# Routing stage written out batch by batch: layer norm three batches ahead over three buffers, squares and lengths earlier

## What is computed

```python
xn = _layernorm(x, ln_gamma, ln_beta)
x_unit = _l2norm(xn, axis=-1)
mu_unit = _l2norm(mu, axis=0)
logits = jnp.einsum('bnd,des->bnes', x_unit * scale, mu_unit)
dispatch = jax.nn.softmax(logits, axis=1)
combine = jax.nn.softmax(logits.reshape(B, N, E * S), axis=-1).reshape(B, N, E, S)
slot_in = jnp.einsum('bnd,bnes->besd', xn, dispatch)
```

## Time and profile before

| what | us |
|---|---|
| three runs: median (lowest, highest) | 1210.41 (1207.87, 1211.22) |
| the profiled execution | 1208.01 |
| its span, first to last instruction | 1206.2 |
| of the span, the routing stage | about 963 to 1110 |

### The profile page before, as it was taken

How to read it: one execution, slowest core, us unless ns; L and a number is a source line. 1 busy time by engine, 2 the same in 40 slices (tenths; PEclk the granted TensorE clock), 3 DMA queues, 4 the chain that set the end, 5 groups by cost and what they waited for, 6 DMA issues and landing times. The chain is left out here.

```text
span 1206.2 us, 28505 instructions
## 1 busy us (share of the span) xinstructions
PE 1040.5 (86%) x8053; PEld 988.6 (82%) x8053; DVE 874.2 (72%) x2292; ACT 748.9 (62%) x2513; POOL 437.8 (36%) x753
## 2 busy tenths in 40 slices
PE   6779999999999998799999926888888747777998
PEld 6679999999999998799999925877787647666877
DVE  4567767777776766677777756999999677776656
ACT  3466666666666665433333307999999547777754
POOL 0132322222332221121121125766777466663015
PEclk9889999999999999899999966999999869999559
DMA  7678960000000000100000035555556010000113
GB/s 230 139 134 226 135 116 0 0 0 0 0 0 0 0 0 1 32 1 0 0 0 0 0 91 139 166 167 151 169 152 174 4 19 1 0 0 4 41 35 122
DMA packets 71575, 73.90 MB, mean 61 GB/s; under 512 B 23025, under 2 KB 63829, under 8 KB 71381
## 3 DMA queue, kind: packets, MB, share of 16 engines
q1 hardware_dynamic: 70692, 72.47, 24.0%
q10 hardware_dynamic: 816, 0.66, 0.2%
HBM read 41.52 MB, written 31.54 MB: 61 GB/s over the span
## 5 line engine op out<-in xcount | busy, mean ns | idle before, releaser
L776 POOL TENSOR_TENSOR att_prob<-att_ex,att_rinv 128x308 f32<-128x308 f32 x128 | 89.9, 702 | 216.1 <-DVE att_rinv L679 202.8
L1056 ACT ACTIVATE att_ex<-att_s_bank,att_mx 128x77 f32<-128x77 f32 x512 | 143.3, 339 | 13.7 <-DVE att_mx L1122 12.1
L1338 ACT ACTIVATE ffn_hid<-ffn_h_bank,ffn_b 128x256 f32<-128x256 f32 x128 | 60.8, 476 | 125.5 <-DVE ffn_hT_lo L1369 65.7
L638 ACT ACTIVATE att_ex<-att_s_bank,att_mx 128x77 f32<-128x77 f32 x512 | 125.0, 333 | 11.5 <-DVE att_mx L669 11.4
L646 ACT ACTIVATE att_qT<-att_q_bank 128x256 f32<-128x256 f32 x128 | 49.2, 385 | 101.0 <-PE att_q_bank L496 99.9
L702 DVE TENSOR_TENSOR att_pT_lo<-att_t_bank,att_pT_hi 128x512 fp32r<-128x512 f32 x128 | 88.3, 691 | 32.1 <-ACT att_pT_hi L616 31.7
L1196 POOL TENSOR_TENSOR att_prob<-att_ex,att_rinv 128x256 f32<-128x256 f32 x128 | 79.8, 623 | 73.1 <-DVE att_rinv L1137 73.1
L516 PE MATMUL att_s_bank<-att_keys,att_qT 128*128 128x154 f32 x512 | 95.0, 309 | 0.0
L616 ACT CAST att_pT_hi<-att_t_bank 128x512 fp32r<-128x512 f32 x128 | 75.0, 587 | 24.2 <-PE att_t_bank L526 19.3
L540 PE MATMUL att_o_bank<-att_pT_hi,att_vals_hi 128*128 128x256 f32 x256 | 82.9, 324 | 3.0 <-DVE att_oT_lo L683 2.0
L1309 PE MATMUL ffn_o_bank<-ffn_w_hi,ffn_hT_hi 128*128 128x256 f32 x256 | 74.5, 291 | 8.0 <-DVE ffn_hT_lo L1369 8.0
(11 more groups left out here) (275 smaller groups left out, 4126.1 us busy)
## 6 DMA issues: line engine op xcount, KB each, us to landing
att_qs<-q_dram SPq DMA_DIRECT2D x96, 128.0 KB, 2.8
ks_dram<-att_zeros SPq DMA_DIRECT2D x16, 462.0 KB, 5.9
att_ks<-ks_dram SPq DMA_DIRECT2D x16, 462.0 KB, 5.2
all_x<-in_x SPq DMA_DIRECT2D x4, 1024.0 KB, 7.7
att_vd<-vd_dram SPq DMA_DIRECT2D x16, 256.0 KB
q_dram<-att_qT_hi SPq DMA_DIRECT2D x16, 256.0 KB, 2.1
q_dram<-att_qT_lo SPq DMA_DIRECT2D x16, 256.0 KB, 2.1
out<-comb_y SPq DMA_DIRECT2D x16, 256.0 KB, 2.1
```

Of the source, the lines that this page charges most:

```text
L638: last = nc.scalar.activation(ex[t % RING][:, r, :], s_bank[t % 2][:, r * SK:(r + 1) * SK], ACT.Exp, bias=mx[t % 2][:, r:r + 1])
L776: nc.gpsimd.tensor_tensor(out, e, w, ALU.mult).then_inc(p_ready, 1)
L1056: last = nc.scalar.activation(ex[t % RING][:, r, :], s_bank[t % 2][:, r * SK:(r + 1) * SK], ACT.Exp, bias=mx[t % 2][:, r:r + 1], **total)
```

## The change

The arithmetic is the same; order, buffers and waits differ.

- No loop: `every_batch` calls a body `batch(f)` for f = 0 to 16 with plain numbers, so each wait is for a constant.
- xa has three buffers (`XR`). In body f, `normalise` and `affine` work on batch f+3 (before: f+2), `statistics` and `inverse_deviation` on f+4 (before: f+3). The stage's head has one more of each, and the inverse of the second length.
- ACT: `square` stands behind the first exponentials instead of the second ones, the copy to moe_comb behind `transposed_x`, `round_x` ahead of the copy to moe_slots.
- DVE: `normalise` stands behind disp_lo instead of ahead of the first maxima; `transposed_x` and the first `weigh` ahead of the second maxima; `statistics` and `invert_length` (of f+2) behind these.
- POOL: `lengths` ahead of `inverse_deviation`. PE: the transposes of x ahead of the second logits.

```diff
-        xa = [m.sb(f"xa{i}", [P, NC, D]) for i in range(2)]
+        XR = 3
+        xa = [m.sb(f"xa{i}", [P, NC, D]) for i in range(XR)]
...
+        def every_batch(eng, body):
+            for f in range(B + 1):
+                body(f)
...
-                if front:
-                    logits(f, i, 1)
-                if following:
+                if f + 1 < B:
                     transpose_x(f + 1)
-                if back:
-                    slot_inputs(f - 1, 1 - i)
+                if f < B:
+                    logits(f, f % 2, 1)
+                if f > 0:
+                    slot_inputs(f - 1, (f - 1) % 2)
...
+            ln.normalise(dve, 2, xg_ready, 1)
+            ln.statistics(dve, 3)
+            invert_length(1)
+            every_batch(dve, batch)
...
-                wait_apart(poolt, xu_ready, NC * (f - 1))
-                wait_apart(poolt, xas_ready, f - 1)
-                nc.gpsimd.tensor_tensor(xa[i][:, :, :], xg[:, :, :], beta[:, :].unsqueeze(1).to_broadcast([P, NC, D]),
+                wait_apart(poolt, xu_ready, NC * (f - 2))
+                wait_apart(poolt, xas_ready, f - 2)
+                nc.gpsimd.tensor_tensor(xa[f % XR][:, :, :], xg[:, :, :], beta[:, :].unsqueeze(1).to_broadcast([P, NC, D]),
                                         ALU.add).then_inc(xa_ready, 1)
...
+            def batch(f):
+                if f < B:
+                    split_x(f, f % 2)
+                if f + 3 < B:
+                    affine(f + 3, 0)
+                if f + 2 < B:
                     lengths(f + 2)
+                if f + 4 < B:
+                    ln.inverse_deviation(pool, f + 4)
...
+            affine(2, 0)
+            ln.inverse_deviation(pool, 3)
+            every_batch(pool, batch)
```

More of the change, by code:

```diff
@@ L1607, in round_x, with batch @@
                 act.wait_ge(xa_ready, f + 1)
-                nc.scalar.copy(xaS[i][0][:, :, :], xa[i][:, :, :]).then_inc(xas_hi, 1)
-            def batch(f, i, front, back, following, later, latest):
+                nc.scalar.copy(xaS[i][0][:, :, :], xa[f % XR][:, :, :]).then_inc(xas_hi, 1)
+            def batch(f):
                 g = f - 1
-                if following:
-                    unit(f + 1, 1 - i)
-                if back:
+                if f + 1 < B:
+                    unit(f + 1, 0)
+                if f > 0:
                     act.wait_ge(t_psum, 2 * g + 1)
@@ L1617, in batch @@
                     nc.scalar.copy(disp[0][:, :, :], t_bank[0][:, :].rearrange("p (q n) -> p q n", q=NC)).then_inc(disp_hi, 1)
-                if front:
+                if f < B:
                     exponentials(f, 0)
-                if back:
-                    act.wait_ge(t_psum, 2 * g + 2)
[L1622 to L1626, removed]
+                if f + 2 < B:
+                    square(f + 2, 0)
+                if f + 1 < B:
+                    transposed_x(f + 1, (f + 1) % 2)
+                if f > 0:
+                    act.wait_ge(t_psum, 2 * g + 2)
+                    nc.scalar.copy(st.comb[:, :, g, :], t_bank[1][:, :].rearrange("p (j n) -> p j n", j=EC)).then_inc(comb_stored, 1)
+                if f < B:
                     exponentials(f, 1)
-                if later:
-                    square(f + 2, i)
-                if back:
+                if f + 1 < B:
+                    round_x(f + 1, (f + 1) % 2)
+                if f > 0:
                     act.wait_ge(i_psum, g + 1)
[L1632 to L1635, removed]
+                    nc.scalar.copy(st.slots[:, :, g, :], i_bank[:, :].rearrange("p (c n) -> p c n", c=DC)).then_inc(slots_stored, 1)
             square(0, 0)
@@ L1752, in split_x, with batch @@
                 wait_apart(poolt, xas_hi, f + 1)
-                nc.gpsimd.tensor_tensor(xaS[i][1][:, :, :], xa[i][:, :, :], fp32_of(xaS[i][0][:, :, :]),
+                nc.gpsimd.tensor_tensor(xaS[i][1][:, :, :], xa[f % XR][:, :, :], fp32_of(xaS[i][0][:, :, :]),
                                         ALU.subtract).then_inc(xas_ready, 1)
[L1756 to L1763, removed]
+            def batch(f):
+                if f < B:
+                    split_x(f, f % 2)
+                if f + 3 < B:
+                    affine(f + 3, 0)
+                if f + 2 < B:
                     lengths(f + 2)
+                if f + 4 < B:
+                    ln.inverse_deviation(pool, f + 4)
             pool.memset(ones[:, :], 1.0).then_inc(const_ready, 1)
```

35 lines of the change are left out of this document (16 added, 19 removed).

## The result

| | before | changed |
|---|---|---|
| median (lowest to highest), us | 1210.41 (1207.87 to 1212.93), 5 runs | 1216.91 (1214.33 to 1222.69), 5 runs |
| ratio to before, 95% interval | | 1.0055, 1.003 to 1.008 |
| the profiled execution; its span | 1208.01; 1206.2 | 1216.08; 1214.3 |

The changed kernel is slower by 0.55%, by more than the 0.3% that a measurement of this kernel can tell from no change. The forecast was 1217, the range 1209 to 1223.

What follows compares the result with a forecast made beforehand. No engine is full; a chain of waits through several engines paces the routing batches. Prologue +3.8, loop and new order +2.6, tail +1.0 sum to +7.4, giving 1217.8 by the median; 1217 us was said, range 1209 to 1223.

Steps and rivals of the forecast that it cites:

- prologue, to unit 2: Head of the routing stage, up to batch 2's scaling of x on ACT: third layer norm delays batch 0, +3.8 us.
- loop written out: Routing stage: twelve batches at the peeled 7.51 us instead of 98.33 in all, order unchanged: -8.2 us.
- new order, twelve batches: Middle of the routing stage: batches take 8.41 us each because the first weighting is held, +10.8 us against written-out batches.
- tail: Last batches of the routing stage, 13 to 15, with allowance for held second weightings: +1.0 us.
- Weighting 0 is held: First weighting of a batch on DVE waits until 0.15 us behind POOL's shift: batch 8.41 us, unheld 7.36.
- a second weighting held by the split: Batches 12 to 14: POOL's split may delay DVE's second weighting, 0 to 0.5 us each, 0.3 taken in all.
- The terms at nothing: Routing parts costed at zero: early squares, third buffer, PE's transposes ahead of second logits, reciprocal deviation last on POOL.
- squares early: ACT's squares behind the first exponentials: removes the 0.80 us wait for the inverse length, costed at nothing.
- its cover of 1.1: Slack between the inverse length being done near 7.3 us and wanted at 8.41; without it the wait returns one for one.
- Not held: Rival: first weighting on DVE runs freely beside POOL's shift, batches 7.36 us, total 1204 us; chance 0.15.
- Weighting 1 held too: Rival: POOL's split also holds the second weighting in every batch, twelve at 8.86 us, total 1223 us; chance 0.07.
- Shorter hand-overs: Rival: first weighting held, but third layer norm gets in first and hand-overs are 0.25 us shorter a batch: 1213; chance 0.12.

Runs made afterwards that it cites:

- the maxima first: Changed kernel with the second maxima put back ahead of the low parts of x and the first weighting on DVE: 1196.52 us, ratio 0.9906; again 1199.14 us.
- the kernel with both edits: Changed kernel with the first softmax's exponentials in PSUM and the second maxima moved ahead of the first weighting on DVE: 1197.04 us, ratio 0.9914 to before.
- the kernel with the squares late: Changed kernel with second maxima ahead of the first weighting, and squares put back behind the second exponentials on ACT: 1209.01 us, ratio 0.9984 to before.

## Why the prediction was right, by its steps

| term, us | forecast | measured | from |
|---|---|---|---|
| prologue, to unit 2 | +3.8 | +3.6 | (993.77 - 970.9) - (991.21 - 971.93) |
| loop written out | -8.2 | -7.8 | 90.50 - 98.33 |
| new order, twelve batches | +10.8 | +10.8 | 101.32 - 90.50 |
| tail | +1.0 | +1.0 | 0.0 + 0.4 + 0.6, below |
| sum | +7.4 | +7.6 | the whole stage on PE, as above: +7.5 |

**Weighting 0 is held.** This was the choice that made the sign, and the nearest row was the right one: the form with one scalar is held like that with two. (The 890 of that row is a mean of two kinds: in the single records a first instruction that meets POOL's addition takes 1.37 to 1.38 and ends 0.15 behind it, the second of its pair takes 0.40.) The written-down layout against the batch from 1019.09:

| since the unit's start | forecast | measured |
|---|---|---|
| layer norm, free | 2.01 to 2.75 | 2.03 to 2.76 |
| POOL scale; shift | 2.82; 4.16 | 2.84; 4.21 |
| weighting starts; ends | 4.2; 5.86 | 4.22; 5.91 |
| second maxima end | 6.46 | 6.51 |
| second exponentials | 6.50 | 6.55 |
| next unit | 8.41 | 8.45 |

The 0.04 that is left comes in between POOL's scale and its shift (1.37 apart instead of 1.34), and everything behind the shift carries it: the end of POOL's instruction is where the batch is tied. The Trainium skill ("GPSIMD Engine Reference", 8. Key points) says that GpSimd contends with DVE instructions in a two-port mode. The trace agrees; how long DVE waits, to 0.15 behind POOL's end, is read off the rows.

**The loop** gave 7.8 of the 8.2 in the experiment: a written-out batch takes 7.54 rather than the 7.51 of the earlier trace rows.

**The prologue.** The third layer norm did wait for the deviation and did meet POOL's split; the weighting of batch 0 then met scale and shift. DVE and POOL there:

```profile
987.17 1.69 DVE L351 TENSOR_SCALAR route_xn<-all_x,route_mean_var,route_rstd 128x256 f32<-128x256 f32 x2 [2.05 <-POOL route_rstd L343]
...
989.50 2.21 DVE L1673 TENSOR_SCALAR route_weight<-route_ex,route_rinv 128x256 f32<-128x256 f32 x2
991.63 0.68 DVE L1662 TENSOR_REDUCE route_top<-route_l_bank 128x2 f32<-128x512 f32 x1
```

```profile
987.10 1.28 POOL L1757 TENSOR_TENSOR route_xaS_lo<-route_xa,route_xaS_hi 128x512 fp32r<-128x512 f32 x1
988.94 1.27 POOL L1738 TENSOR_TENSOR route_xg<-route_xn,route_gamma 128x512 f32<-128x512 f32 x1 [0.55 <-DVE route_xn L351]
990.28 1.28 POOL L1744 TENSOR_TENSOR route_xa<-route_xg,route_beta 128x512 f32<-128x512 f32 x1
```

Normalise 3 (987.17, 1.69) stands in front of batch 0 and is held by the split, which starts 0.07 before it. The pair of the weighting (989.50, 2.21) is held twice, by the scale and by the shift, and ends 0.15 behind the latter.

**The tail** has the right sum from parts of which two were off. Batch 13 takes 7.36 as forecast (1102.45 - 1095.09), batch 14 6.43 to the copy at 1108.88 (forecast 6.40): 0.0 and +0.4. Batch 15 takes 4.50 to the copy at 1113.38, against 3.92 before (1102.95 to 1106.87): +0.6, forecast +0.4. The 0.3 set aside for a second weighting held by the split did not come: those pairs take 0.61 to 0.62. There it is POOL that pays (last section).

**The terms at nothing.** The unit's wait for the inverse is gone, as said. But "squares early" is worth nothing only under a cover, by the forecast that of the held weighting: with it gone (the maxima first) it is worth 0.39 a batch, and there it is still the inverse that the unit waits for. The changed kernel itself with the squares late was not run. The clause that the wait for the inverse would come back if its cover of 1.1 were gone was right in kind; that it comes back one for one was not measured.

**The rivals.** *Not held* (1204): refuted by the 1.69 of the pair, and by the kernel with the exponentials in PSUM, which shows what that case looks like: 7.61 a batch, of which 0.25 is the slower pair itself (0.86 less 0.61), and the rest, 7.36, is what this rival was laid out at. *Weighting 1 held too* (1223): not in the batches of the middle, where it starts at 1026.89 and is done at 1027.50, just ahead of the split at 1027.54; in the tail of the kernel with both edits it did happen. *Shorter hand-overs* (1213): refuted by 8.44.

The median came out as close as it did in part by chance. The sum gave 1217.8, and 1217 was said without a reason for the 0.8. The forecast carried over the 2.4 by which the median of before lies above its profiled execution; the changed kernel's lies 0.8 above its own, and the other stages took 0.6 longer in that.

## What to carry to other kernels

An instruction that runs on one engine can be tied to another engine's instruction without any wait between them in the program; when an order is changed, lay both engines out in time and look for who newly meets whom, with the nearest held pair of the old trace as the price. If the meeting can't be avoided, put nothing behind the held instruction that another engine is waiting for: one line moved ahead of it was worth 1.6 us a batch here (8.44 to 6.87), twice what the hardware loop cost. A step that costs nothing may do so under a cover, and an experiment that takes the cover away gives its price.

## What the hardware showed that was not expected

**A fall of the clock cost nothing in one place and 1.0 us in another.** In the changed kernel PE waits in one piece for the weighting, and behind such a wait its granted clock can fall. Stretches as in the earlier trace rows, and PE's timeline at the end of a wait:

```profile
1012.20:1015.60 3.40, 3.40 (x18) 3.40 (x17) 2.69 (x7) 2.70 (x11) 2.03 (x2) 0.50 0.00 0
1015.60:1029.30 13.70, 10.59 (x84) 9.32 (x83) 10.90 (x31) 9.81 (x32) 9.31 (x13) 1.00 0.01 2
```

```profile
1010.68 0.66 PE L1539 MATMUL route_t_bank<-all_ident,route_weight 128*128 128x128 f32 x4 [1.85 <-DVE route_weight L1673]
```

PE is idle 1.85 us up to 1010.68; from 1012.2 the clock is 0.50, the 1.2 GHz level, for 3.4 us, then 1.00 again for 13.7. There are seven waits of 1.85 in the stage, and behind six of them the clock falls like this; in the batch after a fall PE comes later and waits less (0.69 up to 1019.12). Before, the clock stayed at 1.00 from 986.85 to 1113. The batch with the fall takes as long as the one without, 8.44 (from 1010.65) and 8.45 (from 1019.09), since the second exponentials wait for the held maxima and not for PE. In the kernel with the squares late the same fall, behind an idle time of 1.92, hit the logits that the maxima waited for. The forecast set nothing aside for falls of the clock in the middle of the stage. The sum held because these falls were not on the chain, not because the clock stayed; in this point it was lucky.

**Whoever comes second pays.** In the tail, where no deviation keeps the split back, POOL's split starts while the second weighting is already running. The weighting then takes its usual 0.62, and the split 1.41 instead of 1.27:

```profile
1108.24 0.62 DVE L1673 TENSOR_SCALAR route_weight<-route_ex,route_rinv 128x256 f32<-128x256 f32 x2
```

```profile
1108.59 1.41 POOL L1757 TENSOR_TENSOR route_xaS_lo<-route_xa,route_xaS_hi 128x512 fp32r<-128x512 f32 x1 [5.04 <-ACT route_xaS_hi L1612]
```

The three splits of this kind take 1.39 to 1.41; each starts 0.08 to 0.09 behind the start of a weighting instruction. So a meeting costs POOL about 0.1 when DVE is first by that much, and DVE up to 1.1 when POOL is. When both start within 0.01 of each other, DVE is the one that waits, whichever is first: the weighting at 1006.425 is held (1.43) by a shift that is recorded at 1006.426. Where between 0.01 and 0.07 it turns, and why POOL pays only 0.1, was not tried.
